# Attention on one core: PV of two head groups at a time, behind every second burst of scores

## The reference, cut to what matters

```python
h = jnp.maximum(_layernorm(x, axis=-1), 0.0)
q, k, v = split_heads(h @ Wq.T), split_heads(h @ Wk.T), split_heads(h @ Wv.T)
a = jnp.einsum('bhnd,bhmd->bhnm', q, k) * scale + 2 * adj[:, None]
row_nonzero = jnp.any(a != 0, axis=-1, keepdims=True)
p = softmax(jnp.where(row_nonzero, a, -jnp.inf)), with 0.0 where it is nan
o = jnp.einsum('bhnm,bhmd->bhnd', p, v)
return x + merge_heads(o) @ Wo.T
```

## Time and profile before

| | |
|---|---|
| time, median of 3 runs | 1012.53 us (1010.65 to 1015.43) |
| the profiled execution: its time, its span | 1015.38 us, 1013.6 us |
| mean granted TensorE clock | 0.986 of full speed |
| PE busy | 974.8 us, 96% of the span |
| ACT busy | 927.0 us, 91% |
| POOL busy | 885.2 us, 87% |
| DVE busy | 870.4 us, 86% |

### The profile page before, as it was taken

How to read it: one execution, slowest core, us unless ns; L and a number is a source line. 1 busy time by engine, 2 the same in 40 slices (tenths; PEclk the granted TensorE clock), 3 DMA queues, 4 the chain that set the end, 5 groups by cost and what they waited for, 6 DMA issues and landing times.

```text
span 1013.6 us, 34208 instructions
## 1 busy us (share of the span) xinstructions
PE 974.8 (96%) x11596; PEld 662.7 (65%) x11596; DVE 870.4 (86%) x3218; ACT 927.0 (91%) x3025; POOL 885.2 (87%) x1064
## 2 busy tenths in 40 slices
PE   6798999999999999999999999999999999999976
PEld 5566666667766666776666776666667666666733
DVE  5788988889898888989888898988889988889863
ACT  3399999999999999999999999999999999999992
POOL 1188999999999999999999999999999999999894
PEclk9899999999999999999999999999999999999988
DMA  7078999999999999999999999999999999999996
GB/s 249 11 142 148 183 199 181 182 194 197 180 184 192 191 182 192 174 198 185 197 178 190 194 189 174 198 194 183 183 192 193 178 198 175 196 183 178 165 175 132
DMA packets 569582, 182.62 MB, mean 180 GB/s; under 512 B 542784, under 2 KB 550976, under 8 KB 569408
## 3 DMA queue, kind: packets, MB, share of 16 engines
q1 hardware_dynamic: 569408, 180.43, 97.6%
HBM read 29.36 MB, written 16.78 MB: 46 GB/s over the span
## 4 chain that ended last, share of the span: by engine, by line
PE 74%; DVE 17%; POOL 3%; ACT 3%; issue 2%; DMA 1%; SPq 0%; DVEq 0%; ACTq 0%; POOLq 0%
PE ps L972 48%; PE ps L1044 10%; PE ps L990 9%; DVE logits L687 9%; PE ps L855 4%; PE ps L1018 2%; POOL p L412 2%; DVE some L705 2%; ACT probs L506 1%; DVE o_norm L716 1%; DVE w_max L607 1%; DVE q_lo L749 1%; DMA w_nat<-in_L_gnn_Wq 1%; ACT p L519 1%; PE ps L1055 1%
## 5 line engine op out<-in xcount | busy, mean ns | idle before, releaser
L412 POOL TENSOR_TENSOR p<-probs,p 128x512 f16<-128x512 f32 x512 | 587.7, 1161 | 72.0 <-ACT p L519 68.5
L506 ACT ACTIVATE probs<-logits,row_min 128x256 f32<-128x256 f32 x1024 | 512.1, 509 | 2.6 <-DVE row_min L687 2.6
L687 DVE CUSTOM_DVE_ANT_0 logits<-ps,adj_s,sigma 128x256 f32<-128x256 f32 x1024 | 440.0, 474 | 9.5 <-PE ps L990 9.3
L519 ACT ACTIVATE p<-probs 128x512 f16<-128x512 f32 x512 | 322.0, 629 | 0.0
L972 PE MATMUL ps<-ht_hi,w_hi 128*128 128x256 f16 x1024 | 280.7, 274 | 2.6 <-DVE w_lo L647 1.4
L972 PE MATMUL ps<-ht_lo,w_hi 128*128 128x256 f16 x1024 | 280.1, 274 | 0.0
L972 PE MATMUL ps<-ht_hi,w_lo 128*128 128x256 f16 x1024 | 280.1, 274 | 0.0
L506 ACT ACTIVATION_READ_ACCUMULATOR probs<-logits,row_min 128x1 f32 x1024 | 207.0, 202 | 0.0
L972 PEld LDWEIGHTS ps<-ht_hi,w_hi 128*128 128x128 f16 x1024 | 100.4, 98 | 26.4 <-issue 8.4
L972 PEld LDWEIGHTS ps<-ht_lo,w_hi 128*128 128x128 f16 x1024 | 100.6, 98 | 14.4
L972 PEld LDWEIGHTS ps<-ht_hi,w_lo 128*128 128x128 f16 x1024 | 100.6, 98 | 12.0
(11 more groups left out here) (84 smaller groups left out, 1655.1 us busy)
## 6 DMA issues: line engine op xcount, KB each, us to landing
xs<-in_x SPq DMA_DIRECT2D x32, 512.0 KB, 4.5
out<-xs SPq DMA_DIRECT2D x64, 256.0 KB, 3.3
adj_raw<-in_adj SPq DMA_DIRECT2D x32, 256.0 KB, 3.9
pt<-p SPq DMA_TRANSPOSE x512, 3.5
w_nat<-in_L_gnn_Wq SPq DMA_DIRECT2D x1, 1024.0 KB, 6.8
w_nat<-in_L_gnn_Wk SPq DMA_DIRECT2D x1, 1024.0 KB, 9.3
w_nat<-in_L_gnn_Wv SPq DMA_DIRECT2D x1, 1024.0 KB, 11.4
w_nat<-in_L_gnn_Wo SPq DMA_DIRECT2D x1, 1024.0 KB, 12.9
```

The costliest lines, as they stand in the source:

```text
L412: g.tensor_tensor(p16[:, c % 2, k, 1], probs[:, h % 4].rearrange("p u n -> p (u n)"), p16[:, c % 2, k, 0], ALU.subtract).then_inc(p_split, 1)
L506: e = a.activation(probs[:, h % 4, u, :], logits[:, h % 4, u, :], ACT.Exp, bias=row_min[:, t.par(d), u, h:h + 1], scale=-1.0, accum_out=ro ...
L519: a.activation(p16[:, c % 2, k, 0], probs[:, h % 4].rearrange("p u n -> p (u n)"), ACT.Copy)\
L687: v.tensor_tensor_reduce(out=logits[:, h % 4, u, :], in0=ps[:, S_BANK + h % HC, N * u:N * u + N], in1=adj_s[:, t.par(d), u, :], scale=sigm ...
```

## The change

PV is done for two groups at a time (a pair): behind the bursts of scores of steps 4 and 12 instead of behind every burst. Each visit has 48 matmuls instead of 24, with the semaphore waits for the second group's turned probabilities between the two halves. It writes the whole of bank 4, one half for each group. The row factors of both groups are transposed in one go (four transposes at steps 3 and 11, before: two at 3, 7, 11, 15) into bank 7, where they become two further entries of `AUX_USES`; the copy and the multiplication on VectorE and the two splits on GpSimd are done once a pair, on 128x512 elements. The second `turn_h` moves from step 9 to step 8, and VectorE's `take_h` of it from step 11 to the head of step 10. pt16 gets four groups: groups 2 and 3 are kept in the space of the float32 weights of q and k (`w_nat`), which are not read after the start, as is `norm_t`. In the tail the output projection of the last batch goes by pairs.

```diff
-                need(sp, pv_done, NC * t.batch(d) + (c - 1))
-                sp.dma_start_transpose(pt16[:, c % 2, k], p16[:, c % 2, k].rearrange("p l n -> p (l n)"))\
-                  .then_inc(pt16_in[c % 2][k], 16)
+                need(sp, pv_done, 2 * t.batch(d) + c // 2 - 1)
+                sp.dma_start_transpose(pt(c, k), p16[:, c % 2, k].rearrange("p l n -> p (l n)"))\
+                  .then_inc(pt16_in[c][k], 16)
...
+            def pt(c, k):
+                store = pt16[:, c, k] if c < 2 else w16[:, c - 2, k].rearrange("p (l n) -> p l n", n=P)
+                return store
...
                         (13, ("row", b + 1)), (3, ("norm", b - 1, 1)), (11, ("norm", b, 0))]
                         [(5, ("h", b + 2, 0)), (8, ("h", b + 2, 1))]
...
 GpSimd
-                    if s in (3, 7) and t.prev:
-                        take_o(t, -1, NC - 2 + s // 4)
-                    if s in (11, 15) and t.cur:
-                        take_o(t, 0, s // 4 - 2)
+                    if s == 7 and t.prev:
+                        take_o(t, -1, 1)
+                    if s == 15 and t.cur:
+                        take_o(t, 0, 0)
...
 VectorE
+                    if s == 4 and t.prev:
+                        take_norm(t, -1, 1)
+                    if s == 12 and t.cur:
+                        take_norm(t, 0, 0)
+                    if s == 6 and t.prev:
+                        take_o(t, -1, 1)
+                    if s == 14 and t.cur:
+                        take_o(t, 0, 0)
+                    if later(t, 2) and s == 10 and not t.first:
+                        take_h(t, 2, 1, 2 * t.batch(2) + 2)
...
 TensorE
+            def values(t, d, p):
+                if t is second:
+                    pe.wait_ge(scale_step, 3 * 3 + 1)
+                need(pe, o_ready, 2 * t.batch(d) + p)
+                if p == 0:
+                    for u in range(NU):
+                        pe.wait_ge(pj_taken[u], (NJ // 2) * t.batch(d) + 3)
+                for c in (2 * p, 2 * p + 1):
+                    for k in range(HC):
+                        pe.wait_ge(pt16_in[c][k], 16 * (t.batch(d) + 1))
+                    for mh in range(NU):
+                        for j in range(HC):
+                            o = ps[HD * j:HD * j + HD, PV_BANK, N * (c % 2):N * (c % 2) + N]
+                            h = HC * c + j
+                            for i, (a, b) in enumerate(THREE):
+                                m = mm(o, (v_hi, v_lo)[a][:, t.par(d), mh, HD * h:HD * h + HD],
+                                       pt(c, j)[:, 2 * NU * b + mh:2 * NU * b + mh + NU + 1:NU, :],
+                                       start=(mh == 0 and i == 0), stop=(mh == NU - 1 and i == len(THREE) - 1))
                 m.then_inc(pv_done, 1)
...
                     project(t, s)
+                    if s == 3 and t.prev:
+                        turn_norm(t, -1, 1)
+                    if s == 11 and t.cur:
+                        turn_norm(t, 0, 0)
                     if s % 4 == 0:
                         scores(t, s // 4 + 1)
-                    if s in (0, 4) and t.prev:
-                        values(t, -1, NC - 2 + s // 4)
-                    if t.cur and s >= 8 and s % 4 == 0:
-                        values(t, 0, s // 4 - 2)
+                    if s == 4 and t.prev:
+                        values(t, -1, 1)
+                    if s == 12 and t.cur:
+                        values(t, 0, 0)
...
-                    if t is last and s == 14:
-                        project_last(t, 0, 0)
-                    if t is tail and s in (0, 4, 5):
-                        project_last(t, -1, (1, 2, 3)[s and s - 3])
+                    if t is tail and s in (0, 1, 5, 6):
+                        project_last(t, -1, s if s < 2 else s - 3)
```

More of the change, by code:

```diff
@@ L178, in emit @@
         p_split = sem("p_split")
-        pt16_in = [[sem(f"pt16_in{i}{k}") for k in range(HC)] for i in range(2)]
+        pt16_in = [[sem(f"pt16_in{i}{k}") for k in range(HC)] for i in range(NC)]
         v_hi_ready = sem("v_hi_ready")
@@ L417, in spread_norm @@
                 pool.wait_ge(norm_step, 2 * (NC * t.batch(d) + c) + 2)
-                need(pool, norm_turned, NC * t.batch(d) + (c - 1))
+                pair = 2 * t.batch(d) + c // 2 - 1
+                if pair >= 0:
+                    pool.wait_ge(aux_full, aux_after("norm", pair // 2, pair % 2))
                 wide = [P, NU, HC, HD]
@@ L707, in invert, with take_o, take_norm @@
                  .then_inc(norm_step, 1)
[L709 to L716, removed]
+            def take_o(t, d, p):
+                done = 2 * t.batch(d) + p
+                dve.wait_ge(aux_taken, aux_after("norm", t.batch(d), p))
+                dve.wait_ge(pv_done, done + 1)
+                need(dve, o_split, done)
+                v.tensor_tensor(o_norm[:].rearrange("p c n -> p (c n)"), ps[:, PV_BANK, :], norm_t, ALU.mult)\
                  .then_inc(o_ready, 1)
[L719 to L724, removed]
+            def take_norm(t, d, p):
+                dve.wait_ge(aux_full, aux_after("norm", t.batch(d), p))
+                need(dve, o_ready, 2 * t.batch(d) + p)
+                v.tensor_copy(norm_t, ps[:, AUX_BANK, :]).then_inc(aux_taken, 1)
             def take_probs_t(t, d, c):
@@ L935, in project_last @@
             def project_last(t, d, c):
[L938 removed]
+                pe.wait_ge(o_split, 2 * t.batch(d) + c // 2 + 1)
                 for u in range(NU):
@@ L960, in project @@
                     if j == 6:
-                        pe.wait_ge(o_split, NC * t.batch(0))
+                        pe.wait_ge(o_split, 2 * t.batch(0))
                     if t.first and j in (0, 2, 4):
@@ L1007, in turn_probs @@
                 m.then_inc(aux_full, 1)
-            def turn_norm(t, d, c):
-                pe.wait_ge(norm_ready, NC * t.batch(d) + (c + 1))
-                need(pe, o_ready, NC * t.batch(d) + c)
-                if t is second and c == 0:
-                    pe.wait_ge(scale_step, 3 * 3 + 1)
-                for u in range(NU):
-                    m = tr(ps[:, PV_BANK, N + P * u:N + P * u + P],
-                           norm[:, c % 2, u, :], ident[:])
-                m.then_inc(norm_turned, 1)
@@ L1022, in values, with turn_norm @@
-            def values(t, d, c):
-                for k in range(HC):
-                    if by_dma(HC * c + k):
-                        pe.wait_ge(pt16_in[c % 2][k], 16 * (turns_of(t.batch(d), c, k) + 1))
-                pe.wait_ge(norm_taken, NC * t.batch(d) + (c + 1))
-                if c in Y_C:
-                    pe.wait_ge(aux_taken, aux_after("y", t.batch(d), c))
-                if c == 0:
+            def turn_norm(t, d, p):
+                pe.wait_ge(norm_ready, NC * t.batch(d) + 2 * p + 2)
+                pe.wait_ge(aux_taken, aux_before("norm", t.batch(d), p))
+                for i in range(2):
+                    for u in range(NU):
+                        m = tr(ps[:, AUX_BANK, N * i + P * u:N * i + P * u + P],
+                               norm[:, i, u, :], ident[:])
+                m.then_inc(aux_full, 1)
@@ L1075, in slot @@
                         turn_probs(t, 0, s // 4 - 1)
-                    if s == 3 and t.prev:
-                        turn_norm(t, -1, NC - 1)
-                    if t.cur and s >= 4 and s % 4 == 3:
-                        turn_norm(t, 0, s // 4 - 1)
                     if later(t, 2) and s in turn_h_steps(t):
```

59 lines of the change are left out of this document (18 added, 41 removed).

## The result

| | before | after |
|---|---|---|
| median of 20 runs each | 1013.84 us (1010.65 to 1015.43) | 1010.92 us (1009.12 to 1013.47) |
| profiled execution: time, span | 1015.38, 1013.6 us | 1011.04, 1009.2 us |

After over before is 0.998, 95% interval 0.9971 to 0.999: some 2.9 us faster. The forecast was 7.5 us. The time is inside the range and the direction is right; the gain is well under half of what was worked out, so one step of the working is wrong.

A forecast was written before the change was run, and what follows sets the result against it. PE was taken as the bound (29.54 us a batch) plus a 0.15 stall behind VectorE. Batch 29.69 to 29.33 in 30 slots, -10.8, ends +3.3: -7.5 from median 1012.53, 1005 us; own range 1001 to 1008, outer bounds 999 and 1015.

The forecast's parts named there:

- PE's own work: TensorE's demand a batch: fewer PV visits -0.26, moved transposes -0.05, waits between halves +0.05; 29.54 becomes 29.28 us.
- Rival B: A pair's second half costs a full change of kind, turn_h gives nothing: batch at most 29.53, likelier 1008 us; chance 0.12.
- The third burst's deadline: Step 4's scores wait for VectorE's last logits, ready at +10.6 us after o0, PE at 10.60; stall 0.15 becomes 0.05.
- The edits counted as hidden: Wide take_norm and take_o, take_h, bank 7 waits and transposes: covered by idle time or off the path, no cost.
- Where will they meet GpSimd now?: VectorE's L771 and last L705 stop for GpSimd's instruction under way: L771 0.3 instead of 0.67 us, L705 ends at +9.75.
- nothing in front of L771 changes: On VectorE, L771 starts at +3.21 us after o0 as before, so waits 0.3 us for GpSimd's take_o ending at +3.49.
- VectorE path: VectorE's chain from the end of o0 to the third burst of scores, 11.54 us before; 10.86 without one take_norm and take_o.
- Rival A: VectorE keeps both long stops: path 10.86, stall 0.26, batch 29.54 us, about 1011 us; chance 0.20.
- The ends: Nothing covers the last pair in the tail: +3.3 us taken, from +2.0 to +4.5; the second slot 0.
- the 0.05 of stall that I had kept: The remaining wait of the third burst for VectorE's last logits, 0.05 us a batch, bounds 0 and 0.26.

The follow-up runs named there:

- experiment 4: Changed kernel with GpSimd's split of heads 2 and 3 halved to 256 of 512 columns from the fifth batch on; 1002.58 us, 0.9912 of before.
- experiment 5: `a_pool`: changed kernel with neg_mean and var_s moved from VectorE to GpSimd, ahead of its rstd; 1004.16 us, 0.9914 of before.
- experiment 2: Kernel before, with the first q_lo on VectorE moved to the end of step 2, ahead of mean and variance; 1019.48 us, 1.0083 of before.
- experiment 6: Kernel before, with neg_mean and var_s moved from VectorE to GpSimd; 1025.93 us, 1.0133 of before.
- experiment 1: Changed kernel with the first q_lo on VectorE moved to the end of step 2, ahead of mean and variance; 1014.3 us, 1.0019 of before.
- experiment 8: Changed kernel with GpSimd's take_o as four 128x256 instructions a pair instead of two of 128x512; 1024.11 us, 1.0114 of before.
- experiment 3: Kernel before, unchanged, traced once more; one time, 1013.36 us. Window columns: stretch, us, busy of PE, PEld, DVE, ACT, POOL, granted clock, DMA share, GB/s.

## Why the prediction was right or wrong

**PE's own work: right.** Forecast 29.28 us a batch; measured 29.50 - 0.28 = 29.22, and 29.21 in the three versions without the stall. The last full batch, in which VectorE has no layer norm of a later batch, gives both demands by itself: 29.52 before and 29.21 after, -0.31 where -0.26 was forecast. Scores to projection is 0.21. Between the halves of a pair the distance from start to start is 0.11 (519.27 to 519.38), as within a half. Rival B is out.

**The third burst's deadline: right, in part by luck.** Counted from the end of o0 (521.63, 0.04 ahead of residual as before), the burst starts at +10.87, and at +10.59 without the stall in front of it; PE's part was forecast at 10.60. The last L708 ends at +9.78, forecast +9.75: it took 0.42 and not over 0.7, since it came later into the same split. But from there to the burst the rows of before have 0.93 (535.45 to 536.38), where the working took 0.81 and 0.05. With q_lo in time and all else as it is, the burst would have waited some 0.12 (an estimate, 9.78 + 0.93 against 10.59) and not 0.05. It waits 0 because PE comes to it late. In experiments 4 and 5, where PE comes on time, this instruction (L709 there) ended earlier, at +9.3 and +8.8, and the burst waits 0.

**The edits counted as hidden: right.** Neither the transposes nor bank 7 nor h shows among PE's waits of the steady part; q_hi's idle time on ScalarE is gone, and k_hi has 0.71 us.

**"Where will they meet GpSimd now?": wrong.** This is the failed step. "They" were L771 and the last L705; the phases were worked out for the two instructions that had stopped in the trace of before, and not for those that had not. By the same numbers neg_mean, at 533.93 - 524.84 = 9.09 us before, would come at 9.09 - 0.68 - 0.35 = +8.06, and GpSimd's three splits were forecast to end at +8.55: a stop of some 0.5, to be had from the rows in hand. From its start to the next it measured 0.49, and this is what makes q_lo late. The first L705, at 526.87, had started just as GpSimd's o_hi ended (526.48 + 0.41). Counted from the end of o0, it starts at +2.03 in both kernels, but o_hi now begins 0.17 later and lasts 0.20 longer, and catches it: +0.30. So "nothing in front of L771 changes" was wrong too: it comes at +3.49 and not +3.21, and stops for 0.13 where 0.3 was forecast.

**The path was followed to the wrong end.** I took the third burst as the only deadline of the VectorE path. The job of step 4, which needs the bank of q_lo, starts 1.56 us earlier (534.82 against 536.38) and had 0.01 us of slack. Removing 0.79 us of PE's work in front of it asked 0.79 of VectorE; it gave 0.51. The forecast of stops alone would have given 1.03 and been in time.

Rival A (29.54, 1011) has nearly the measured time, and not its mechanism: L771's stop all but went, L775 taking 0.21, the last L708 took 0.42, and the wait is not at the third burst. That its number fits is luck.

**The ends: right in size, as far as can be told.** Forecast +3.3. From the third burst of the 29th full slot to the end, the four traces with PV by group (before, its copy, experiments 2 and 6) take 91.21, 89.17, 91.67 and 90.51 us, mean 90.6; the four with pairs and wide splits (after, experiments 1, 4 and 5) 93.09, 93.71, 93.2 and 94.89, mean 93.7: +3.1. The last full batch is in these figures; without it the difference is +3.5. PE's waits from 950 us to the end, by the list of waits, add up to 12.0 to 12.9 us in the first four and 14.5 to 15.2 in the second four. Between the two traces of the result the 4.3 us for transposes are gone, and those for GpSimd's o_lo went from 3.1 to 11.0. No experiment undid the pair in the tail alone, so how much of this is the pair's and how much the phase of the last slot stays open. In the two profiled executions the ends differ by 1.88 only: each lies 0.6 us from the mean of its four.

The sum then, in the three pieces of the table: the starts, which spread over 3 to 4 us among either four, differ by -0.3 in the mean; 28 x -0.19 is -5.3; the end is +3.1. That is -2.5 us, against -2.9 measured. Missing are 0.17 us a batch, 5 us in all. Experiments 4 and 5 get them back, and 0.12 a batch more (29.21 against the forecast's 29.33): the 0.05 of stall that I had kept, and 0.07 of PE's work.

## What to carry to other kernels

When work is taken from the bounding engine, every deadline behind it moves up by that much. This holds for deadlines that are just met too, which have no row in the list of waits: check for each buffer that the engine claims how long ago the other engine let go of it. Where VectorE and GpSimd stop each other, follow every small VectorE instruction that works in SBUF alone through GpSimd's new timetable, not only those that stop now, or move them away from VectorE. And before a cure is carried to another version, look who waits for the engine that takes the work.

## What the runs showed of the hardware

- The duration of neg_mean, a VectorE instruction on 2 elements a partition, was 0.17, 0.57, 0.98 or 1.11 us, by how much was left of a GpSimd instruction of 1.16 us beside it; var_s, of the same size, took 1.17 in experiment 8. Halving the GpSimd instructions alone brought 0.57 down to 0.17 (experiment 4).
- A move that changes no work, of one instruction by 0.6 us, cost 0.21 us a batch (experiment 2); the same engines and instructions with GpSimd 0.4 us later cost 0.35 (29.50 to 29.85).
- The granted clock of TensorE changes within the tail. In the changed kernel, PE waited 4.54 us and ran its next 12 matmuls at half clock (1.2 GHz); it waited 2.83 us ahead of the last 12 and ran them at full clock (2.4 GHz). In `a_pool`, after the same two waits, the first 12 came back to full clock after seven, and the last 12 fell to half at the fifth: from start to start 0.22 became 0.40 to 0.43 us. Windows of the changed kernel, then of `a_pool` (columns as in experiment 3):

```profile
992.60:997.80 5.20, 5.08 (x12) 1.87 (x13) 0.00 (x0) 0.00 (x0) 1.74 (x3) 0.50 0.65 123
...
1003.00:1006.00 3.00, 2.76 (x12) 1.09 (x12) 0.70 (x2) 0.00 (x0) 0.01 (x1) 1.00 0.02 5
```
```profile
994.40:997.40 3.00, 3.00 (x9) 0.93 (x7) 0.68 (x1) 0.00 (x0) 0.00 (x0) 0.50 0.00 0
```

By these distances 12 matmuls at half clock instead of full cost 12 x 0.21 = 2.5 us (an estimate). Between the two traces of before the ends differ by 2.04 us, of the 4.8 us over which that kernel's 20 times spread.
